# The attention sums of a seven-layer transformer stack with the probabilities as weights and v as the moving operand

## The reference, cut to what matters

```
q, k, v = split_heads(h @ Wq), split_heads(c @ Wk), split_heads(c @ Wv)   # c: h, or the context
s = einsum('bhqd,bhkd->bhqk', q, k) * 8 ** -0.5                        # causal mask in L0 and L2 self
p = softmax(s)
o = einsum('bhqk,bhkd->bhqd', p, v)                                     # the part that changes
x = x + merge_heads(o) @ Wo + bo                                        # before or after it a norm
```

## Time and profile before

| | |
|---|---|
| median of 3 runs | 2332.77 us (2331.26 to 2337.57) |
| profiled execution, its own time | 2326.22 us |
| its span, first to last instruction | 2323.9 us |
| mean granted TensorE clock | 0.981 of full speed |
| TensorE busy | 2108.6 us |
| VectorE, ScalarE, GpSimd busy | 1829.7, 1647.3, 1384.1 us |
| first scores (L790) begin | 57.6 us after the span's start |

### The profile page before, as it was taken

The page is one execution under the profiler, slowest core; times in us unless marked ns, Lnnn a source line. Parts: engine busy times, 40 slices in busy tenths (PEclk is TensorE's granted clock), DMA queues, the critical chain, the costliest instruction groups (busy, mean ns, idle before and its releaser), DMA issues.

```text
span 2323.9 us, 100781 instructions
## 1 busy us (share of the span) xinstructions
PE 2108.6 (91%) x40685; PEld 1726.2 (74%) x40685; DVE 1829.7 (79%) x4657; ACT 1647.3 (71%) x3278; POOL 1384.1 (60%) x3557
## 2 busy tenths in 40 slices
PE   2789989899999998999999998989999999899987
PEld 2577867687888776777888787768788877677765
DVE  3589887787888887777888888778788889877764
ACT  0367756687887775777888775668788777577775
POOL 3355446886555444888555544688655544488843
PEclk6899999999999999999999999999999999999999
DMA  6355555454555555544555555544455545554432
GB/s 149 91 135 135 134 134 133 113 120 117 131 133 127 136 136 136 125 115 114 133 131 133 129 134 139 131 118 120 117 133 129 123 120 123 136 127 114 120 95 58
DMA packets 310571, 289.18 MB, mean 124 GB/s; under 512 B 50080, under 2 KB 251552, under 8 KB 310112
## 3 DMA queue, kind: packets, MB, share of 16 engines
q1 hardware_dynamic: 305120, 279.80, 48.9%
q10 hardware_dynamic: 4128, 1.65, 0.4%
q0 software_dynamic: 864, 1.28, 0.3%
HBM read 130.51 MB, written 34.60 MB: 71 GB/s over the span
## 4 chain that ended last, share of the span: by engine, by line
PE 48%; POOL 20%; SPq 10%; DVE 7%; ACT 6%; issue 5%; DMA 4%; DVEq 1%; POOLq 0%; ACTq 0%
PE ps_scores_t L837 7%; PE ps_scores L790 6%; PE ps_turn L891 6%; PE ps_turn L821 6%; SPq L531 6%; PE ps_wide L919 5%; PE ps_turn L896 3%; POOL x L645 2%; DVE row_max L1145 2%; PE ps_wide L916 2%; DMA k_slots<-k_dram 2%; PE ps_wide L866 2%; PE ps_wide L867 2%; PE ps_wide L873 2%; POOL post_rstd L603 2%
## 5 line engine op out<-in xcount | busy, mean ns | idle before, releaser
L1145 DVE TENSOR_REDUCE row_max<-ps_scores 128x16 f32<-128x1024 f32 x448 | 547.4, 1222 | 306.3 <-PE ps_scores L790 139.3
L1151 DVE TENSOR_TENSOR shifted<-ps_scores,row_max 128x512 f32<-128x512 f32 x896 | 598.7, 686 | 15.4
L731 ACT ACTIVATE probs<-ps_scores_t 128x512 f32<-128x512 f32 x896 | 486.3, 595 | 79.7 <-PE ps_scores_t L837 77.6
L721 ACT COPY pv_sb<-ps_turn 128x256 f32<-128x256 f32 x448 | 167.0, 373 | 361.5 <-PE ps_turn L821 357.1
L790 PE MATMUL ps_scores<-k_slots,qk_rows 32*64 32x256 f32 x7168 | 311.4, 403 | 49.7 <-DMA k_slots<-k_dram 43.5
L821 PEld LDWEIGHTS ps_turn<-probs,v_ones 128*32 128x32 f32 x14336 | 222.0, 110 | 151.7 <-ACT turned L702 75.9
L837 PE MATMUL ps_scores_t<-ident,shifted 64*128 64x64 f32 x7168 | 321.5, 230 | 11.4 <-DVE attn L1163 7.7
L837 PEld LDWEIGHTS ps_scores_t<-ident,shifted 64*128 64x128 f32 x7168 | 260.0, 140 | 54.9 <-ACT turned L702 9.3
L821 PE MATMUL ps_turn<-probs,v_ones 128*32 128x64 f32 x14336 | 294.7, 223 | 4.2 <-ACT turned L702 2.0
L702 ACT COPY turned<-ps_turn 128x256 f32<-128x256 f32 (+2 forms) x466 | 192.2, 412 | 125.5 <-PE ps_turn L954 111.1
L726 ACT ACT_TABLE_LOAD x190 | 243.8, 1283 | 3.3
(11 more groups left out here) (172 smaller groups left out, 4539.9 us busy)
## 6 DMA issues: line engine op xcount, KB each, us to landing
v_ones<-v_rows SPq DMA_DIRECT2D x1792, 64.0 KB, 2.3
k_slots<-k_dram SPq DMA_DIRECT2D x448, 256.0 KB, 3.3
k_dram<-qk_rows SPq DMA_DIRECT2D x448, 64.0 KB, 2.8
x_in<-in_x SPq DMA_DIRECT2D x64, 64.0 KB, 2.0
ctx_in<-in_ctx SPq DMA_DIRECT2D x64, 64.0 KB, 2.0
out<-x SPq DMA_DIRECT2D x64, 64.0 KB, 1.8
k_dram<-zeros SPq DMA_DIRECT2D x4, 256.0 KB, 6.0
w<-in_L_xattn_W SPq DMA_DIRECT2D x2, 256.0 KB, 6.4
```

The lines of the kernel that those rows point to most:

```text
L731: nc.scalar.activation(probs[:, b, :, :], ps_scores_t[:, b, :] .rearrange("p (h t) -> p h t", t=LEN), ACT.Exp, scale=SCALE).then_inc(probs ...
L1145: v.tensor_reduce(row_max[:, :].rearrange("p (g n) -> p g n", n=SLOTS), ps_scores[:, :, 0:256].rearrange("p g (n k) -> p g n k", k=LEN), A ...
L1151: v.tensor_tensor(shifted[:, j % 2, u, :].rearrange("p (g n k) -> p g n k", n=SLOTS, k=LEN), ps_scores[:, 2 * u:2 * u + 2, 0:256].rearrang ...
```

## The change

The probabilities of a head pair (128 rows, 64 columns) become the weights and `v_ones` (32 columns) moves. The result lands with the queries down the partitions, as the next step wants it, in `ps_scores_t`, 32 columns for each head pair. ScalarE's copy, `pv_sb` and the two transposes per unit are gone. The values move from behind the scores to the end of the phase, ahead of the up part, and there they are those of unit j - 1; the turn of `attn` and the projection come one phase earlier. The diff, without declarations and removed functions (the three functions `phase` in it are ScalarE's, TensorE's and VectorE's, in this order):

```diff
-VALUES, TURN_OUT, OUT = 2, 3, 4
+VALUES, TURN_OUT, OUT = 1, 2, 3
...
                 def phase(r, j):
-                    if exists(r, j - VALUES):
-                        copy_pv(r, j - VALUES)
                     if exists(r, j - 1):
                         exps(r, j - 1, 0)
...
                 def values(r, j):
                     f = j % FAR
                     pe.wait_ge(v_landed[f].sem, v_landed[f].at(r, j))
                     pe.wait_ge(probs_ready.sem, probs_ready.at(r, j))
-                    for u in range(HALVES):
+                    for n in range(HEADS // 2):
                         for b in range(SEQS_OF_PAIR):
-                            for h in range(4):
-                                ins = nc.tensor.matmul(ps_turn[32 * h:32 * h + 32,
-                                                               u * P + 64 * b:u * P + 64 * b + 64],
-                                                       v_ones[:, f, b, 4 * u + h, :],
-                                                       probs[:, b, 4 * u + h, :], start=True, stop=True)
+                            ins = nc.tensor.matmul(ps_scores_t[64 * b:64 * b + 64, 0, n * V_COLUMNS:(n + 1) * V_COLUMNS],
+                                                   probs[:, b, n, :], v_ones[:, f, b, n, :], start=True, stop=True)
...
                 def transposes(r, j):
-                    if exists(r, j - VALUES):
-                        pe.wait_ge(attn_ready.sem, attn_ready.at(r, j - VALUES))
+                    pe.wait_ge(attn_ready.sem, attn_ready.at(r, j - 1))
...
                 def phase(r, j):
                     if exists(r, j):
                         scores(r, j)
+                    if exists(r, j - 1):
+                        transposes(r, j - 1)
                     turned_free(r, j)
                     if not turned_parts(r, j - 1):
                         residuals_read(r, j - 1)
-                    if exists(r, j - VALUES):
-                        values(r, j - VALUES)
-                    if exists(r, j - 1):
-                        transposes(r, j - 1)
-                    if exists(r, j - VALUES):
-                        pv_taken(r, j - VALUES)
+                    if exists(r, j - OUT):
+                        project(r, j - OUT)
                     if has_mlp(r, j - DOWN):
                         mlp_down(r, j - DOWN)
-                    if exists(r, j - OUT):
-                        project(r, j - OUT)
                     if exists(r, j + QKV):
                         qkv(r, j + QKV)
-                    if exists(r, j - VALUES):
-                        pv_t(r, j - VALUES)
                     if turned_parts(r, j):
                         turns(r, j)
                     if exists(r, j + QKV) and layer_of(j + QKV) == L1_CROSS:
                         rope_v(r, j + QKV)
+                    if exists(r, j - VALUES):
+                        values(r, j - VALUES)
                     if has_mlp(r, j - UP):
                         mlp_up(r, j - UP)
...
                 def normalise(r, j):
-                    dve.wait_ge(pv_t_ready.sem, pv_t_ready.at(r, j))
+                    dve.wait_ge(pv_ready.sem, pv_ready.at(r, j))
...
                 def residual(r, j):
                     dve.wait_ge(y_ready.sem, y_ready.at(r, j))
+                    dve.wait_ge(mlp_y_ready.sem, mlp_y_ready.at(r, j + OUT - DOWN))
...
                 def phase(r, j):
+                    if exists(r, j - VALUES - 1):
+                        normalise(r, j - VALUES - 1)
                     if exists(r, j):
                         maxima(r, j)
-                    late = has_mlp(r, j - DOWN)
-                    if exists(r, j):
+                    down = has_mlp(r, j - DOWN)
+                    if down and exists(r, j):
                         shift(r, j, 0)
-                        if late:
-                            shift(r, j, 1)
-                    if late:
-                        mlp_residual(r, j - DOWN)
                     if exists(r, j - OUT):
                         residual(r, j - OUT)
-                    if exists(r, j) and not late:
+                    if down:
+                        mlp_residual(r, j - DOWN)
+                    elif exists(r, j):
+                        shift(r, j, 0)
+                    if exists(r, j):
                         shift(r, j, 1)
...
                     if rope:
                         rope_products(r, j + QKV)
-                    if exists(r, j - VALUES):
-                        normalise(r, j - VALUES)
                     if rope:
                         rope_sum(r, j + QKV)
```

More of the change, by code:

```diff
@@ L256, in build @@
         probs = sb("probs", [P, SEQS_OF_PAIR, HEADS // 2, LEN])
-        pv_sb = sb("pv_sb", [P, HALVES, P])
         recip = sb("recip", [P, HEADS])
@@ L297, in build @@
         pv_ready = signal("pv_ready")
-        pv_t_ready = signal("pv_t_ready")
         y_ready = signal("y_ready")
@@ L717, in copy_rope_v @@
                         .then_inc(rope_v_ready.sem, 1)
-                def copy_pv(r, j):
-                    act.wait_ge(pv_ready.sem, pv_ready.at(r, j))
-                    nc.scalar.copy(pv_sb[:, :, :], ps_turn[:, 0:256].rearrange("p (u t) -> p u t", u=2)) \
-                        .then_inc(pv_copied.sem, 1)
                 def gelus(r, j):
@@ L951, in turns @@
                     if exists(r, j - TURN_OUT):
-                        if not exists(r, j - VALUES):
-                            pe.wait_ge(attn_ready.sem, attn_ready.at(r, j - TURN_OUT))
+                        pe.wait_ge(attn_ready.sem, attn_ready.at(r, j - TURN_OUT))
                         ins = nc.tensor.transpose(ps_turn[:, 256:384], attn[:, (j - TURN_OUT) % 2, :], ident[:, :])
```

13 lines of the change are left out of this document (removed).

## The result

The changed kernel takes **2362.2 us** (median of 4 runs, 2359.92 to 2366.05), the kernel before in the same rounds 2332.02 (2330.41 to 2337.57): a ratio of 1.0127 with an interval of 1.0103 to 1.015, so 30 us or 1.3% slower. Forecast was slower, by 90. The profiled span grew from 2323.9 to 2358.3 us; the mean granted clock is 0.983 against 0.981. The means hide a small difference. In the kernel before TensorE waits 2.73 us for GpSimd's norm (`POOL x L645`) up to 458.47 us, and from 457.8 to 464.6 the granted clock is 0.5 (1.2 GHz) where it is 1.0 (2.4 GHz) on either side. Behind the first 106 us of the run there are seven such stretches, 27 us in all, six at a wait of 2.7 to 3.1 us ahead of the MLP's turn and one at a wait of 1.97 us for k. The loads in them take 5.1 us longer than their like. The changed kernel has no such stretch from 116 to 2351 us.

What follows compares the result with a forecast made beforehand. TensorE's program order was taken to bound. 237 - 99 + 38 - 70 - 57 - 45 + 15 + 36 + 15 + 12 + 8 = +90 on 2326.2 us gave 2416, as median 2423 us; range 2345 to 2490.

Steps and rivals of the forecast that it cites:

- Values (+237): TensorE's values piece: 16 waves paced by the 64-column load, 1.12 us instead of 0.59 in 448 units, +237 us.
- pace 0.056: Rival for the values: loads of two column tiles follow without the 7 ns, piece 1.02, 2378 us; chance 0.17.
- ScalarE's copy of the sums: nothing by itself: Removing ScalarE's copy gains nothing: ScalarE has 29% free and TensorE waits for it elsewhere.
- Transposes of the sums (-99): Removing the two transposes of `pv_sb` from TensorE's path saves 0.22 us in each of 448 phases, -99 us.
- (1): Up phases: values between full-size pieces add a change of tile shape, +0.20 us x 192 = +38 us.
- (2): Up part comes a values piece later, covering its wait for the read of `ps_wide`: -70 us.
- (3): Projection and residual come a phase earlier, so GpSimd has two phases for the norm before the MLP's turn: -57 us.
- (6): Down phases: turns wait for both residuals, behind projection, down and one shift, about 0.1 x 128 = +12 us.
- (4): Scores' waits for k: phases longer by 0.3 us cover them, -45 of the 54 us.
- (5): Transposes wait for `attn`: +15 after phases without up part or mask, +36 with rope and down, +15 with three norms.
- (7): First and last 16 phases: only every other unit is there and exp is no longer hidden, +8 us.
- (8): Values wait for the same phase's exps: taken as nothing, covered by only 0.07 us; each 0.1 beyond costs 45 us.

Runs made afterwards that it cites:

- experiment 3: The changed kernel with 14 of the 16 value matmuls of a unit streaming 64 columns instead of 32, same result: 2361.34 us, ratio 1.0125.
- experiment 1: The kernel before with probabilities as weights and v moving, values in the old place, copy and two transposes kept: 2458.87 us, ratio 1.0549.
- experiment 7: The changed kernel with the projection between the scores and the transposes: 2422.76 us, ratio 1.0396.

## Why the prediction was right in sign and too high

**Values (+237): the mechanism held, the size was off.** Load sets the pace (experiment 3), 16 waves, constant as taken. The step that failed is "I take 0.0625, the pace of the row that has two tiles too". In the loads of the changed kernel successive waves start 0.058 apart ((1.01 - 0.14) / 15), so the piece is 1.055 and not 15 x 0.0625 + 0.18 = 1.1175, and 0.0625 x 448 = 28 us of the forecast go. Small terms (0.584 and not 0.59 before, four pieces at the lower clock after) take back 4, which leaves +213 for the swap itself. The +203 of the account holds another step that failed, "ScalarE's copy of the sums: nothing by itself": in 17 units TensorE waited for that copy, 10 us that are gone. The row that I chose has the same number of tiles, but they are row tiles of 64 rows with 128 columns each; the load I had worked out by itself, 0.054, was nearer. (On the queue these loads last 138 ns, not 131; the 131 were loads of 32 rows.) The rival "pace 0.056" rested on just this and had the chance 0.17. With this term right the sum would have been +62, still twice what was measured; the rest is in (5) and in the small waits below. The rules: TensorEngine Tiling (Array Packing), "When to Use Tiling", in the Trainium skill, spoke against the swap, and experiment 1 agrees (+128 us for the form alone). The rule of another page of the Trainium skill, TensorE: Matmul & The Clock Gate, "Part 3: Packing small matmuls" (a load overlaps streams only of other row groups), would have made the piece 1.54, an estimate from it and the rows before; the trace disagrees, with 1.055.

**Transposes of the sums (-99): right**, -97 and 5 of waits.

**(1) Change of shape (+38): right**, +34.

**(2) Up part (-70): right**, -65, and experiment 1 shows that it is the place that does it: 75 us stay where the form changes and the place doesn't.

**(3) and (6) Turns (-57 + 12): right in sum, and that is luck**: -31.9 - 13.5 = -45 against -45. (3) holds: waits of over 0.6 us ahead of the MLP's turn sum to 55 us before, and there is none now. But (6) cost 24 us there and not 12. The turn now waits in most of the 192 down phases, 0.15 us on average, for the two residuals behind a shift:

```profile
1160.06 0.30 PEld L860 LDWEIGHTS ps_wide<-w_v,turned 128*128 128x128 f32 x2
1160.07 0.28 DVE L1160 TENSOR_TENSOR x<-ps_turn,x_bias 128x128 f32<-128x128 f32 x1
...
1160.42 0.14 PEld L910 LDWEIGHTS ps_turn<-ident,mlp_normed 128*128 128x128 f32 x1
```

Without a wait L910 would start at 1160.28, 0.22 behind L860. What made it up is the turn of a layer's input, which the sum had at nothing and which waits 13.5 us less.

**(4) k (-45): measured -35**, 10 less. Of the same kind is what the phases no longer wait for in small: -13 in "all others", which the sum had at nothing; up to 5 of it is the clock (see the result) and not cover.

**(5) and (7) `attn` (+66 + 8): measured +54.** Right in its place, oversized in its largest term. The 40 phases with rope and down cost 18.9 us, not 36: 12 of them are late by 0.84, as the earlier trace rows let expect (0.9), but 20 by 0.38 and 8 by 0.14. One such stretch had stood for all. The 128 phases without rope and masks, taken at 15, were 80 phases of down without a mask at 12.8 together with another 15 in phases without an MLP. The 32 with two norms in one list were 3.3 instead of 15. The first 16 phases cost 7 more, as (7) had it, though part of that can be the clock: from 55 to 120 us of the span it is 0.74 on average, against 0.82 before.

**(8) The exps (0): right.** 3.9 us of waits for `probs`, covered as thinly as said: experiment 7 took 0.2 of that cover away and paid 40 us.

In sum: forecast +90, measured +30 by the runs and +34 by the account. Too dear were the values by 24 and ScalarE's copy by 10, `attn` with the thin ends by 20, the small waits by 18 (with those of the transposes of the sums), and (1) by 4; too cheap were k by 10, (2) by 5 and small pieces of work by 5: 76 - 20 = 56. The large errors lay on one side: I took the dearer value for the pace and for `attn`, and nothing at all for small waits that a longer phase covers.

Still open: whether four tiles would reach their 0.7 us pieces without the gaps, that is whether code loading makes them. No run tried a program with the same work and fewer instructions.

## What to carry to other kernels

Before operands of small matmuls are swapped, count loads and streams per wave and time the one that is longer, from a row with the same kind of tile (rows and columns), not only the same number of tiles: in float32 it was a load of 64 columns against a stream of 64, and the swap doubled the waves. A layout change that saves a step pays if the saved step costs more than the piece grows: 0.22 us saved against 0.47 in float32, against 0.13 in bfloat16. Once one engine's pieces follow each other without a gap, price an edit with the waits that it covers or uncovers: here three quarters of the net work (108 of 142 us, or 118 of 152 with the copy's wait) was given back that way.

## What the runs showed of the hardware

- Column tiles of 128 rows overlap loads and streams as freely as row tiles do: with two tiles a wave of float32 loads of 64 columns starts every 0.058 us (0.0615 to 0.0625 for the row tiles of the transposes, with 128 columns each), with streams of 32 or of 64 columns hidden behind it.
- A full-size piece between tiled pieces costs 0.2 us more than among its like, at each place: 0.31 against 0.11 for the last turn, 0.42 against 0.22 for the projection. 448 such places were worth 89 us.
- Float32 loads of 32 columns on four column tiles take 0.70 us for the work for which two of 64 take 1.055, but with stalls of up to 1.5 us inside a piece, with nothing waited for, that end 1.3 to 1.6 us after a packet of instructions has landed (430 packets against 318). That the packets cause them isn't shown.
- Bfloat16 turns two passes into one (7168 loads instead of 14336): the piece of 16 matmuls went from 1.055 to 0.36 us, that of the old form from 0.58 to 0.23.
